# A four-engine woven pipeline for sparse graph attention: steps written out instead of looped, their order rewoven, and the mean row moved from VectorE to GpSimd

## What is computed

```python
h = jnp.maximum(_layernorm(x, axis=-1), 0.0)
# in _L0_gnn_ref(h, adj, ...):
q = (h @ Wq + bq).reshape(b, m, 8, 64); k, v likewise
scores = einsum('bmhd,bnhd->bhmn', q, k) / 8 + transpose(edge_bias[edges], (0, 3, 1, 2))
scores = leaky_relu(scores, 0.2)
scores = where(edges > 0, scores, -1e9)
out = einsum('bhmn,bnhd->bmhd', softmax(scores), v).reshape(b, m, 512)
x + out @ Wp + bp
```

## Time and profile before

| | before |
|---|---|
| median of three executions | 1049.67 us |
| the profiled execution | 1053.46 us, of which the span is 1051.7 us |
| TensorE (PE) busy | 94% of the span |
| VectorE (DVE) busy | 87% |
| ScalarE (ACT) busy | 74% |
| GpSimd (POOL) busy | 47% |
| mean granted TensorE clock | 0.985 |

### The profile page before, as it was taken

How to read it: one execution, slowest core, us unless ns; L and a number is a source line. 1 busy time by engine, 2 the same in 40 slices (tenths; PEclk the granted TensorE clock), 3 DMA queues, 4 the chain that set the end, 5 groups by cost and what they waited for, 6 DMA issues and landing times.

```text
span 1051.7 us, 32494 instructions
## 1 busy us (share of the span) xinstructions
PE 989.4 (94%) x9056; PEld 974.2 (93%) x9056; DVE 917.3 (87%) x3409; ACT 779.8 (74%) x1737; POOL 493.6 (47%) x865
## 2 busy tenths in 40 slices
PE   5568999999999999999999999999999999999995
PEld 4458999999999989999999999999999999999995
DVE  4958899889998989989999869989998999989984
ACT  3567887788778877787777757788878877878762
POOL 1003444554455445554554434455455544545454
PEclk9998999999999999999999979999999999999998
DMA  7574434434344434434343433434434353534220
GB/s 171 177 223 121 115 113 133 116 107 139 110 132 115 115 116 117 125 105 139 114 135 104 123 95 113 133 96 125 133 107 146 86 149 101 142 106 120 70 75 9
DMA packets 190794, 125.52 MB, mean 119 GB/s; under 512 B 32832, under 2 KB 180300, under 8 KB 190604
## 3 DMA queue, kind: packets, MB, share of 16 engines
q1 hardware_dynamic: 189812, 122.75, 40.7%
q10 hardware_dynamic: 792, 0.53, 0.2%
HBM read 79.19 MB, written 44.04 MB: 117 GB/s over the span
## 4 chain that ended last, share of the span: by engine, by line
PE 64%; DVE 21%; issue 8%; ACT 2%; DMA 1%; DVEq 1%; POOL 1%; ACTq 0%; SPq 0%; POOLq 0%
PE bank L1232 14%; PE bank L1263 8%; PE bank L1185 7%; PE bank L1322 6%; PE bank L1220 6%; PE bank L1174 5%; DVE w L1678 5%; PE bank L1175 4%; PE bank L1209 4%; PE bank L1197 4%; PE bank L1240 3%; DVE onehot L1690 3%; DVE q_lo L1652 2%; DVE w L1701 2%; DVE o_all L1777 2%
## 5 line engine op out<-in xcount | busy, mean ns | idle before, releaser
L1039 POOL TENSOR_SCALAR a_line<-w,a_bias 128x256 f32<-128x256 f32 x512 | 261.8, 511 | 459.8 <-DVE w L1701 416.0
L1232 PE MATMUL bank<-pt,nat_sb 128*65 128x128 f32 x2048 | 267.2, 274 | 0.2
L1678 DVE CUSTOM_DVE_ANT_0 w<-bank,mask_rows 128x256 f32<-128x256 f32 x512 | 195.7, 419 | 60.2 <-PE bank L1175 41.4
L1456 ACT ACTIVATE pt<-bank 128x512 f32<-128x512 f32 x256 | 153.8, 601 | 118.0 <-PE bank L1185 113.6
L1701 DVE SCALAR_TENSOR_TENSOR w<-w,shift,a_line 128x256 f32<-128x256 f32 x512 | 231.2, 491 | 7.1 <-issue 4.6
L1232 PEld LDWEIGHTS bank<-pt,nat_sb 128*65 128x65 f32 x2048 | 232.4, 139 | 0.6 <-issue 0.6
L1690 DVE TENSOR_TENSOR onehot<-val,counts_to 128x512 fp32r<-128x512 f32 x256 | 176.5, 689 | 9.8 <-DVE val_max L1645 9.2
L1438 ACT ACTIVATE mask_own<-bank,mask_bias 128x512 bf16<-128x512 f32 x256 | 174.8, 683 | 1.4 <-PE bank L1209 1.4
L1185 PE MATMUL bank<-ident,w 128*128 128x128 f32 x1024 | 154.9, 274 | 0.0
L1447 ACT ACTIVATE t_sb<-bank 128x512 fp32r<-128x512 f32 x256 | 150.1, 586 | 3.2 <-PE bank L1197 3.0
L1174 PE MATMUL bank<-t_sb,q_hi 128*128 128x256 f32 x512 | 144.3, 303 | 5.8 <-issue 4.7
(11 more groups left out here) (135 smaller groups left out, 1634.3 us busy)
## 6 DMA issues: line engine op xcount, KB each, us to landing
adj_in<-in_adj_dram SPq DMA_DIRECT2D x64, 512.0 KB, 4.0
mask_store<-mask_own SPq DMA_DIRECT2D x64, 512.0 KB, 3.3
mask_rows<-mask_store SPq DMA_DIRECT2D x512, 64.0 KB, 2.4
nl_store<-nl_ring SPq DMA_DIRECT2D x7, 512.0 KB, 4.2
stack_store<-stage SPq DMA_DIRECT2D x7, 512.0 KB, 3.1
h_stack<-stack_store SPq DMA_DIRECT2D x7, 512.0 KB, 5.1
h_nl<-nl_store SPq DMA_DIRECT2D x28, 128.0 KB, 3.6
x_res<-in_x_dram SPq DMA_DIRECT2D x16, 128.0 KB, 2.2
```

Of the source, the lines that this page charges most:

```text
L1039: nc.gpsimd.tensor_scalar(a_line[:, i % 2, :], w[:, i, :], 5.0, a_bias[:, i:i + 1], ALU.mult, ALU.add)\
L1232: last = pe.matmul(o_part[0:D + 1, P * u:P * u + P], nat_sb[:, t % 2, p % 4 * 2 + u, k, :], pt[:, p % 2, u, k, :], start=(k == 0), stop=(k ...
L1678: nc.vector.tensor_tensor_reduce(w[:, i, :], row_bank[:, SLOTS * u:SLOTS * u + SLOTS], mask_rows[:, t % 2, p % 4 * 2 + u, :], 0.25, LEAST_ ...
```

## The change

1. The loops are gone: all engines run `for b in range(B): for s in range(K0, K0 + PPG)` as straight code.
2. `norm`'s first half no longer adds the mean row. `add_heads` on GpSimd does: one multiplication into a new tile `vec_share` (128x64), one addition into `x_res`, both ahead of the sums of the heads.
3. TensorE's order within a step: `turn_y` and `weigh` go behind `natural`; the projection is no longer a block of its own, its four products stand one behind each of the four products of `weigh`. ScalarE's order follows.
4. Lags: `COUNT` 6 to 7, `USED` 7 to 8, the two halves of the projection from 27 and 28 to 28 and 30 (steps D and B), of `norm` from 28 and 29 to 29 and 31 (steps A and C), `SUM` 30 to 32 (from step B to step D), `OUT` 31 to 33.
5. VectorE takes counts, flags, ranks and the first half of beta ahead of the scores.

```diff
-    LOAD, CONV, TURN_A, COUNT, USED, RANK, VAL, ONEHOT = 0, 4, 5, 6, 7, 8, 9, 9
+    LOAD, CONV, TURN_A, COUNT, USED, RANK, VAL, ONEHOT = 0, 4, 5, 7, 8, 8, 9, 9
-    SCORE, A_LINE, Y, TURN, PV, X_ADD, PROJ, NORM, SUM, OUT = 17, 19, 20, 21, 22, 24, 27, 28, 30, 31
+    SCORE, A_LINE, Y, TURN, PV, X_ADD, PROJ, NORM, SUM, OUT = 17, 19, 20, 21, 22, 24, 28, 29, 32, 33
@@ every engine
-            with sp.Fori(0, B // 2 - 1) as i:
-                for odd in range(2):
-                    for s in range(K0, K0 + PPG):
-                        step(2 * i + odd, s)
-            for s in range(K0, K0 + PPG):
-                step(B - 2, s)
-            for s in range(K0, K0 + PPG):
-                step(B - 1, s)
+            for b in range(B):
+                for s in range(K0, K0 + PPG):
+                    step(b, s)
@@ GpSimd, add_heads
+                pool.wait_ge(alone_ready, n + 1)
+                if t % TPG == 0:
+                    pool.wait_ge(vec_ready, b + t // TPG + 1)
+                if t % MT == 0:
+                    pool.wait_ge(x_added, 2 * b + t // MT + 1)
+                pool.nop(nofuse=True)
+                nc.gpsimd.tensor_scalar(vec_share[:, :], vecs[:, bass.ds(D * b + D * (t // TPG), D)], alone[:, 0:1], 0.0,
+                                        ALU.mult, ALU.add).then_inc(vec_added, 1)
+                pool.wait_ge(vec_added, n + 1)
+                nc.gpsimd.tensor_tensor(row, row, vec_share[:, :], ALU.add).then_inc(share_added, 1)
                 pool.wait_ge(proj_taken, 2 * n + 2)
-                pool.wait_ge(vec_added, n + 1)
@@ TensorE, weigh
+                if due is not None:
+                    free(adj_bank_uses, b, s, len(list(adj_bank_uses(b, s))) - 1)
                 for u in range(2):
                     for k in range(2):
                         last = pe.matmul(o_part[0:D + 1, P * u:P * u + P], nat_sb[:, t % 2, p % 4 * 2 + u, k, :],
                                          pt[:, p % 2, u, k, :], start=(k == 0), stop=(k == 1))
-                last.then_inc(pv_done, 1)
+                        if (u, k) == (1, 1):
+                            last.then_inc(pv_done, 1)
+                        if due is not None:
+                            project(b, *due, 2 * u + k)
@@ VectorE, norm
-                if e == 0:
-                    dve.wait_ge(alone_ready, n + 1)
-                    if t % TPG == 0:
-                        dve.wait_ge(vec_ready, b + t // TPG + 1)
-                    if t % MT == 0:
-                        dve.wait_ge(x_added, 2 * b + t // MT + 1)
-                    nc.vector.scalar_tensor_tensor(x_res[:, t // MT % 2, t % MT, :], vecs[:, bass.ds(D * b + D * (t // TPG), D)], alone[:, :],
-                                                   x_res[:, t // MT % 2, t % MT, :], ALU.mult, ALU.add)\
-                        .then_inc(vec_added, 1)
```

More of the change, by code:

```diff
@@ L1222, in natural, with weigh @@
                 last.then_inc(nat_done, 1)
-            def weigh(b, p):
+            def weigh(b, p, due, s):
                 n, t = PPG * b + p, p // 4
@@ L1270, in step @@
                     scores(b, p)
-                p = pair(b, s, TURN)
[L1272 to L1276, removed]
                 due = piece(b, s, TFILL, 4)
@@ L1285, in step @@
                     natural(b, p)
+                p = pair(b, s, TURN)
+                if p is not None:
+                    turn_y(b, p)
+                p, due = pair(b, s, PV), piece(b, s, PROJ, 2, 2)
+                if p is not None:
+                    weigh(b, p, due, s)
+                elif due is not None:
+                    wait_projection(b, *due, s)
+                    for h in range(4):
+                        project(b, *due, h)
                 t = tile(b, s, TURN_A)
@@ L1291, in step @@
                     count(b, t, s)
-                due = piece(b, s, PROJ, 2)
-                if due is not None:
-                    project(b, *due, s)
                 i = 0
@@ L1349, in _ @@
                     turn_graph(k)
-            with pe.Fori(0, B // 2 - 1) as i:
-                for odd in range(2):
-                    for s in range(K0, K0 + PPG):
-                        step(2 * i + odd, s)
-            for s in range(K0, K0 + PPG):
-                step(B - 2, s)
-            for s in range(K0, K0 + PPG):
-                step(B - 1, s)
+            for b in range(B):
+                for s in range(K0, K0 + PPG):
+                    step(b, s)
             pe.wait_ge(kinds_known, 1)
@@ L1532, in _ @@
                     settle(act)
-            with act.Fori(0, B // 2 - 1) as i:
-                for odd in range(2):
-                    for s in range(K0, K0 + PPG):
-                        step(2 * i + odd, s)
-            for s in range(K0, K0 + PPG):
-                step(B - 2, s)
-            for s in range(K0, K0 + PPG):
-                step(B - 1, s)
+            for b in range(B):
+                for s in range(K0, K0 + PPG):
+                    step(b, s)
             act.wait_ge(kinds_known, 1)
@@ L1705, in step @@
                     take_counts(b, t)
+                t = tile(b, s, USED)
+                if t is not None:
+                    flag_used(b, t)
+                t = tile(b, s, VAL)
+                if t is not None:
+                    take_ranks(b, t)
+                due = beta_piece(b, s, BETA + 1)
+                if due is not None:
+                    pick_beta(b, *due)
                 p = pair(b, s, SCORE)
@@ L1723, in step @@
                     low_q(b, *due)
-                t = tile(b, s, VAL)
-                if t is not None:
-                    take_ranks(b, t)
                 four = p is not None and p % 2 == 1
@@ L1821, in _ @@
                     settle(dve)
-            with dve.Fori(0, B // 2 - 1) as i:
-                for odd in range(2):
-                    for s in range(K0, K0 + PPG):
-                        step(2 * i + odd, s)
-            for s in range(K0, K0 + PPG):
-                step(B - 2, s)
-            for s in range(K0, K0 + PPG):
-                step(B - 1, s)
+            for b in range(B):
+                for s in range(K0, K0 + PPG):
+                    step(b, s)
             dve.wait_ge(kinds_known, 1)
```

39 lines of the change are left out of this document (22 added, 17 removed).

## The result

The changed kernel takes 1064.11 us (median, 1063.79 to 1064.44), the kernel before 1049.68 beside it: a ratio of 1.0106, 95% interval 1.0063 to 1.0149. The forecast of 1035.0 had the wrong sign, and its range of 995 to 1060 doesn't hold the time. The profiled execution took 1064.11 us with a span of 1062.3.

The account below looks back on a forecast made before the run. TensorE was taken as full, VectorE nearly in step with it. From the median 1049.67: jumps -7.1, straight graphs -2.1, the tile on the circle through GpSimd -6.4, the end +1.5, giving 1035.6, rounded 1035; range 995 to 1060.

Parts of the forecast that it names:

- Straight code: All engines' loops written out: two jumps go, -7.1 us, and six graphs run 0.35 us faster each, -2.1.
- The circle: GpSimd's block, VectorE's norm, TensorE's steps to scores of C, VectorE back: 11.06 us + X, tile 14.48, -6.4 us over 64 tiles.
- block X: GpSimd's mean row plus adding in step D: 0.75 + 2.67 = 3.42 us, between 2.70 and 4.02.
- Once-a-graph work: Operations done once a graph, 12.3 and 8.3 us over 64 tiles: about 0.3 us a tile.
- The base of comparison: Kernel before: ordinary tile 14.58 us, TensorE alone needing 14.28, VectorE with 0.94 us to spare in step D.
- the first rival: Weave comes through: tile falls to TensorE's floor of 13.86, time 996; 20% with its surroundings, below 1011.
- The weave: Projection products between `weigh`'s on TensorE: intervals 111 and 56 ns in turn, 0.21 us per projection, -0.42 a tile.
- VectorE loses L1773: VectorE no longer adds the mean row in norm: 0.26 to 0.30 us a tile less.
- The end: `SUM` two steps later lengthens the kernel's tail: +1.5 us, between 0 and +3.
- Slower by GpSimd: GpSimd becomes the bound and the kernel gets slower than before; slower had 14%.
- the second rival: Full exclusion between GpSimd and VectorE: X = 4.27, tile 15.33, +48 us, time 1088; slower had 14%.
- Its turning point: GpSimd's block from X = 3.75 on: +14.6 us eat the straight code's gain, tile 14.81.

Follow-up runs that it names:

- the pads: Changed kernel with an idle GpSimd memset ahead of GpSimd's block: 1076.02 us with 128x512, 1109.94 us with 128x1280.
- `after`: The changed kernel itself, with the whole change against the kernel before: 1064.11 us, ratio 1.0106.
- the pads on a later kernel: 128x256 VectorE memset added to the 1020.76 us kernel (adding in step B, row on VectorE): before norm's multiplication 1031.58, step B 1020.67, behind step A's one-hot block 1023.25.
- the best kernel: Changed kernel with two `o_all` and two `alone`, GpSimd's adding back in step B and the mean row on VectorE: 1020.76 us, ratio 0.9696.
- the run without the weave: Changed kernel with two `o_all`, adding back in step B, and projections behind `weigh`'s four products: 1036.28 us, against 1025.48 with the weave.

## Why the prediction was wrong

**Straight code: right.** No branch is left in TensorE's trace, no inner graph of the straight code alone is above 119.7 us, and the part alone gave a ratio of 0.989, where 1040.5 is 0.991 of 1049.67.

**The circle: the mechanism was right, and its sum is the step that failed.** `norm` waits for GpSimd's `x_res` (39.8 us) and L1249 for `o_all` (48.3 us, 0.75 a tile), as foretold, and the pads show that the block counts in full. But the forecast had the tile at 14.48, 0.10 below a plain tile of the kernel before; measured, a plain tile is 0.25 above it (14.59 to 14.84) and the mean tile 0.47 (14.87 to 15.34). Measured over nine tiles of 556 to 690 us, against the terms:

```
                                   forecast   measured
L1705 to conversion, conversion      2.93       2.92
block X                              3.42       3.54
summed to L1249                      0.99       1.19  (1.09 in eight of nine)
L1249 to scores of C                 4.32       4.66  (4.32 in four of the nine, 4.54 in one)
scores of C to L1705 of D            2.82       3.05
tile                                14.48      15.36
```

The forecast's 14.48 is a plain tile, for the 0.3 us of once-a-graph work was taken off on both sides; so 0.3 of the 0.88 between the two sums was no miss. In the five of the nine tiles without the large operations of once a graph (14.70 to 14.94; the four with them take 15.61 to 16.48) the terms are short as follows:

- *The block*: 3.56 on average in these five, 0.14 too small. The size came from the right row, but not all of its cause: `vec_share`, priced at 0.32 to 0.38, took 0.72 on average over all tiles, and the three sums took 1.90, less than the 2.21 of step B.
- *Handovers*: `summed` to L1249 took 1.09 and not 0.99.
- *Scores of C to L1705 of D*: 2.91 and not 2.82.
- *Once-a-graph work*: taken as 0.3 us a tile, equal in both kernels. The mean tile is 0.28 above a plain one in the straight code and 0.50 in `after`. On the circle it makes 0.34 us in step B and 0.14 in VectorE's step C, over the nine tiles.

So of the 0.57 us by which the mean tile missed its forecast change, 0.35 is the plain tile and 0.22 the once-a-graph work.

**The base of comparison: right in size, wrong in reading.** The 14.58 for a plain tile of before fits the straight code's 14.59. But I took it for TensorE's own tile, with 0.3 us of open time, and thought that VectorE had spare time in step D. By the segments above, the second circle runs through that tile, and VectorE's idle time of 0.94 us in step D is the stretch in which it waits for TensorE on that circle. That it was no spare time is argued here, from the pads on a later kernel; no pad was put on the kernel before. The floor of the first rival, 13.86, was not far off: with no wait for GpSimd, the best kernel's plain tile takes 14.02. What kept that kernel 25 us above the rival's 996 is in part this 0.16 a tile, in part the once-a-graph work, which there makes 0.57 us a tile instead of 0.3.

**The weave: right, in kind and size.** Matmuls of the changed kernel in a woven stretch:

```profile
742.32 0.33 PE L1272 MATMUL bank<-w_ext,ot_sb 65*128 65x65 f32 x2
...
742.49 0.38 PE L1238 MATMUL bank<-pt,nat_sb 128*65 128x128 f32 x2
```

Four instructions, two of each kind, take 0.39 us. The intervals behind the projection's are 60 and 110 ns in turn, where the forecast had 56 and 111. A step with the weave costs 0.69 us more than one without a projection (1.56 and 0.87 for the stretch), and the forecast had 0.89 - 0.21 = 0.68, against 0.91 for the block of the straight code. The circle's term with the weave in it, L1249 to the scores of C, is 4.32 in plain tiles as foretold. The 0.155 of the run without the weave is smaller for another reason: there the block stands right behind `weigh`, its first interval is already 61 ns and the others 110 to 112, so weaving turns three long intervals into short ones and not four. Only the projection in step B is on TensorE's part of the second circle; from the scores of D on the circle runs over VectorE. The two together would be worth 0.31 us a tile, 20 us; the experiment says 10.8, about one of them (0.155 x 64 is 9.9).

**VectorE loses L1773: wrong.** I priced it at 0.26 to 0.30 us a tile. In `norm` it was worth 0.05 to 0.15 (`den` to the end of `o_all` 0.88, 0.92 and, in the straight code, 0.98 with it, 0.83 without). Part of its time is one in which VectorE waits for its own reciprocal anyway: in the timeline above `den` starts at 585.96 and `o_all` at 586.46, 0.50 later, where it is 0.40 without the row (746.19 and 746.59). Moved to GpSimd, with the block in step B, it costs VectorE more than that: operations beside it get longer. VectorE's busy time in two inner graphs is 221.5 us with the row on GpSimd and 218.4 with the row on VectorE; the windows of those graphs:

```profile
308.85:426.47 117.62, 115.78 (x1113) 113.41 (x1112) 110.71 (x407) 94.14 (x210) 66.55 (x122) 1.00 0.42 123
```

```profile
307.93:424.49 116.56, 115.00 (x1113) 113.45 (x1112) 109.44 (x415) 94.13 (x210) 60.99 (x106) 1.00 0.42 124
```

The group of `shift` (count, busy us, mean ns) from 308 to 662 us, first with the row on GpSimd, then without:

```profile
L1751 DVE SCALAR_TENSOR_TENSOR shift<-wmax,shift_neg 128x4 f32<-128x4 f32 x49 | 16.8, 344 | 0.0
```

```profile
L1741 DVE SCALAR_TENSOR_TENSOR shift<-wmax,shift_neg 128x4 f32<-128x4 f32 x48 | 11.9, 248 | 0.0
```

**The end: +1.5 forecast, 2.1 measured** (the stretch from the last graph's first scores to the end went from 131.8 to 133.9).

**The rivals.** Slower by GpSimd, with 14% of the chances, is what came, but not by the second rival's path: it asked for a block of 4.27, over 3.8 at the least, and `w` waiting for `a_line`; measured are 3.54 and 10.7 us of such waits in the whole span. That its tile of 15.33 is the mean tile measured, 15.34, is luck, since it had no once-a-graph work in it. Its turning point, X = 3.75, was too high for the reasons above: with X = 3.54 the kernel was already slower. Even by the forecast's own terms it should have been about 3.64, where the gain of 9.2 less the 1.5 of the end is used up.

Its price, 4.27, rested on whether GpSimd's and VectorE's operations exclude each other, and there I misread the trace: L1030 and L1701 have overlapping records, and I took that for less than exclusion. A record includes the time that the operation waits inside. The clearest pairs stand in the trace of the kernel with the block in step B and the row on VectorE, here first with GpSimd a little ahead, then with VectorE a little ahead:

```profile
568.94 0.74 POOL L1054 TENSOR_TENSOR x_res<-x_res,out_const 128x256 f32<-128x256 f32 x1
```

```profile
569.00 1.23 DVE L1684 TENSOR_TENSOR onehot<-val,counts_to 128x512 fp32r<-128x512 f32 x1
```

```profile
510.71 1.24 POOL L1054 TENSOR_TENSOR x_res<-x_res,out_const 128x256 f32<-128x256 f32 x1
```

```profile
510.68 0.68 DVE L1684 TENSOR_TENSOR onehot<-val,counts_to 128x512 fp32r<-128x512 f32 x1
```

The one-hot block, 0.68 us elsewhere, takes 1.23 in the first and ends 0.55 behind GpSimd's addition: it did its work almost wholly after it. In the second it keeps its 0.68, and the addition takes 1.24 and ends 0.59 behind it. All fourteen such meetings of this trace are of these two kinds, seven of each, and the later one pays. In the timeline of `after` L1025 (0.31 alone) ends 0.1 behind the one-hot block although its record starts 0.05 before that one's, so a record's start alone doesn't tell who is first; and the pair of L1705 is 0.57 longer beside the sums.

This fits the Trainium skill, "SBUF — State Buffer", section "Who interferes with whom": a VectorE instruction with two SBUF inputs contends with a GpSimd one that reads SBUF, the pair of ports that they share is an exclusive lock, the order of issue decides who is blocked, and a GpSimd instruction that only writes isn't contended with (the memset's 523 to 529 ns agree). So the rule held; what was wrong in 4.27 is that GpSimd would pay for every collision. In `after` VectorE pays 0.57 us of L1705 itself.

**The loss as a sum** (from the traces of the straight code alone and of `after`): the span went from 1037.6 to 1062.3 us, by 24.7. Of that the six inner graphs make 22.3 (712.7 to 735.0), the tail 2.8 (131.1 to 133.9), and the start -0.4.

What stays open: how much of the remaining loss each single collision makes. The overlap was moved and lengthened, never taken away alone, and no run changed where the operands lie. The earlier counts, flags, ranks and beta, and the place of `turn_y` and `weigh` behind `natural`, were never tried apart from the rest; whether they cost or gain is not shown.

## What to carry to other kernels

Before moving work, close the circle of the kernel as it is: follow it from one instruction to its next instance across engines, piece by piece, and see that each piece starts where the one before it ends; then test a piece with an operation whose result nobody reads. Work of once a graph belongs into it with its place, not as a mean taken off on both sides. Idle time in which an engine waits for the circle need not be spare time, and an engine's work counts on its stretch of the circle: the same 0.27 us were worth 10.8, 0 and 2.5 us at three places. A small operation that runs in part while its engine waits for its own predecessor is nearly free (0.05 to 0.15 us of 0.26 to 0.30 here), so moving it to an engine whose operations collide with the first one's can cost as much as it took. Where a consumer moves closer to its producer, look first at the queue of the producer: swapping two neighbours there, or a second buffer and the old place, took back all of the loss here, and the latter with the row left on VectorE gave 1020.76 us, 3% below the kernel before (ratio 0.9696).

## What the runs showed of the hardware

- A record's duration includes waiting for the other engine: GpSimd's multiplication of 128x64 takes 0.31 us alone and 0.84 beside VectorE's one-hot block (0.722 on average over 64); a GpSimd memset of 0.53 us at the same place keeps its speed (523 to 529 ns in all 64, 50 of which run beside a one-hot block).
- When GpSimd's addition of 128x256 and VectorE's one-hot block start within 0.06 us of each other, one keeps its time (0.73 or 0.68) and the other takes 1.23 or 1.24; seven meetings of each kind in one trace.
- VectorE's operations on 4 columns take 0.15 us alone and up to 0.71 beside GpSimd's additions, so a trace's minimum for them says nothing of their price at another place.
- Matmuls of 65 columns with 128-column weight loads (the projection) follow one another every 112 ns in a block of their own. In pairs, each behind a pair of matmuls of 128 columns with 65-column loads (`weigh`), the intervals behind them are 60 and 110 ns in turn.
